# Maxima rows and evacuation moved behind the next round's first exponentials, in the first attention of a two-layer gated cross-attention block

## What is computed

```python
qkv = x @ w_attn + b_attn;  kv_ctx = context_seq @ w_ref + b_ref
key = concat([kc, k], axis=1);  value = concat([vc, v], axis=1)
w = einsum('bhtd,bhsd->bhts', qh, kh) / sqrt(Dh)
...
probs = softmax(w, axis=-1)
a = einsum('bhts,bhsd->bhtd', probs, vh)
```

## Time and profile before

| | |
|---|---|
| median of 3 runs | 696.75 us (691.8 to 701.3) |
| the profiled execution | 700.24 us, span 698.5 us |
| PE busy | 514.7 us (74%) |
| DVE busy | 437.9 us (63%) |
| ACT busy | 298.5 us (43%) |
| mean granted TensorE clock | 0.869 |

### The profile page before, as it was taken

How to read it: one execution, slowest core, us unless ns; L and a number is a source line. 1 busy time by engine, 2 the same in 40 slices (tenths; PEclk the granted TensorE clock), 3 DMA queues, 4 the chain that set the end, 5 groups by cost and what they waited for, 6 DMA issues and landing times. The chain is left out here.

```text
span 698.5 us, 15585 instructions
## 1 busy us (share of the span) xinstructions
PE 514.7 (74%) x5425; PEld 355.1 (51%) x5425; DVE 437.9 (63%) x918; ACT 298.5 (43%) x480; POOL 146.5 (21%) x184
## 2 busy tenths in 40 slices
PE   0381778879878988844537798989975158999994
PEld 0161345556556655733223365655554146788883
DVE  7724577666656676456962676777567873666652
ACT  1065324555555555502404265766753221333331
POOL 1200002111211121100032601112123032444432
PEclk9995968999999897877868788999986578999998
DMA  8030683444534550000044559699447111222310
GB/s 259 4 112 3 117 161 78 127 106 106 124 77 100 145 145 24 2 0 1 0 113 81 150 144 179 138 167 161 136 156 254 54 38 17 42 43 44 51 23 0
DMA packets 73247, 64.31 MB, mean 92 GB/s; under 512 B 33326, under 2 KB 65750, under 8 KB 73190
## 3 DMA queue, kind: packets, MB, share of 16 engines
q1 hardware_dynamic: 61816, 41.78, 26.4%
q0 software_dynamic: 8224, 21.06, 11.6%
q10 hardware_dynamic: 3152, 0.71, 0.5%
HBM read 48.59 MB, written 15.92 MB: 92 GB/s over the span
## 5 line engine op out<-in xcount | busy, mean ns | idle before, releaser
L458 PE MATMUL PS<-QS,KS 112*120 112x100 f16 (+2 forms) x896 | 93.0, 230 | 11.2 <-ACT PT L521 9.5
L458 PEld LDWEIGHTS PS<-QS,KS 112*120 112x120 f16 (+2 forms) x896 | 82.4, 144 | 36.6 <-ACT PT L521 15.1
L569 DVE CUSTOM_DVE_ANT_0 PS<-PS,maskv 100x461 f32<-100x461 f32 x128 | 80.4, 647 | 13.9 <-PE PS L427 12.6
L572 DVE TENSOR_REDUCE mx<-PS 100x1 f32<-100x361 f32 x128 | 63.6, 529 | 37.0 <-PE PS L430 35.8
L521 ACT ACTIVATE PT<-PS 120x400 f32<-120x400 f32 (+1 forms) x128 | 63.3, 503 | 37.1 <-PE PS L458 34.8
L521 ACT ACTIVATE PT<-PS,ctxb 120x400 f32<-120x400 f32 (+1 forms) x96 | 56.9, 594 | 49.8 <-PE PS L458 48.5
L427 PE MATMUL PS<-KS,QS 65*100 65x461 f16 x128 | 51.6, 408 | 15.6 <-DVE mx L569 15.1
L2003 PE MATMUL PS<-WE,hidden_high 128*128 x160 | 55.4, 391 | 5.7 <-issue 5.7
L1990 PE MATMUL PS<-aT,WE 128*128 128x128 f16 x960 | 59.3, 221 | 0.0
L779 POOL TENSOR_SCALAR_AFFINE_SELECT PT<-PT 100x400 f32<-100x400 f32 x32 | 17.7, 554 | 190.8 <-ACT PT L521 190.8
L1990 PEld LDWEIGHTS PS<-aT,WE 128*128 x960 | 56.6, 99 | 0.5
(11 more groups left out here) (302 smaller groups left out, 1062.3 us busy)
## 6 DMA issues: line engine op xcount, KB each, us to landing
share<-in_L_ffn_w_dram POOLq DMA_DIRECT2D x13, 1024.0 KB, 8.5
k_scratch<-share SPq DMA_DIRECT2D x32, 180.5 KB, 2.5
KS<-k_scratch SPq DMA_DIRECT2D x32, 180.5 KB, 3.7
KS<-k_scratch SPq DMA_DIRECT2D x64, 90.2 KB, 5.8
QS<-q_scratch SPq DMA_DIRECT2D x64, 50.0 KB, 2.6
v_scratch<-xn SPq DMA_DIRECT2D x8, 385.7 KB
values_staged<-v_scratch SPq DMA_DIRECT2D x8, 385.7 KB
WE<-in_L_ffn_w_dram POOLq DMA_DIRECT2D x2, 1024.0 KB, 8.8
```

Of the source, the lines that this page charges most:

```text
L458: last = nc.tensor.matmul(bank[0:kn, i * T:(i + 1) * T], KS[p][:, h, k0:k0 + kn], QS[p][:, h, :], start=True, stop=True)
L569: nc.vector.tensor_tensor_reduce(rows, rows, maskv[:, :], 1.0, -BIG, ALU.add, ALU.max, mx[p][:, h:h + 1]).then_inc(s_smf, 1)
L572: nc.vector.tensor_reduce(mx[p][:, h:h + 1], sm_bank[h % 2][0:T, 0:TC], X, ALU.max).then_inc(s_smf, 1)
```

## The change

On ACT the maxima rows of twelve heads move behind the next round's exp0 and the evacuation behind its exp1. `NTURN0` goes from 2 to 3, so that PE's turn and DVE's division stand one step later, and T1 goes from step 3 to step 2 on PE, ACT and DVE (in rounds 0 to 5). ACT's loop gets the form that PE's and DVE's have. No computation is added or removed.

```diff
-        TVK = {1: "T0", 3: "T1", 4: "K0", 5: "K1", 8: "V0", 9: "V1", 11: "K2", 12: "K3"}
+        TVK = {1: "T0", 2: "T1", 4: "K0", 5: "K1", 8: "V0", 9: "V1", 11: "K2", 12: "K3"}
...
-        NTURN0 = 2
+        NTURN0 = 3
...
-                def round0(j, u, keys, nxt, weights=False):
+                def round0(j, u, keys, nxt, first=False, weights=False):
                     nh0 = MISC0 + MISCR * (2 * j + u)
                     for t in range(16):
                         act_exp(act, j, u, t, 0, 0)
+
+                        if t == 0 and not first:
+                            act_max_rows(act, j, u, 1, 0)
+                        if t == 1 and not first:
+                            act_evac(act, j, u - 1, 0)
                         if weights and 1 <= t < 1 + NIB + KC:
                             rounding(NIB + t - 1)
...
                     if nxt:
                         act_max_rows(act, j, u + 1, 0, 0)
-                    act_evac(act, j, u, 0)
-                    if nxt:
-                        act_max_rows(act, j, u + 1, 1, 0)
-
-                with act.Fori(0, B // 2 - 1) as j:
-                    for u in range(2):
-                        round0(j, u, True, True)
+
+                round0(0, 0, True, True, True)
+                with act.Fori(0, B // 2 - 2) as j:
+                    round0(j, 1, True, True)
+                    round0(j + 1, 0, True, True)
+                round0(B // 2 - 2, 1, True, True)
                 round0(B // 2 - 1, 0, False, True)
-                round0(B // 2 - 1, 1, False, False, True)
+                round0(B // 2 - 1, 1, False, False, False, True)
+                act_evac(act, B // 2 - 1, 1, 0)
```

## The result

The changed kernel takes 694.17 us (median of 20 runs, 689.72 to 701.5), the kernel before 699.57 in the same comparison (20 runs, 691.8 to 703.03). The ratio is 0.9947 [0.9921, 0.9972]: 2.0 to 5.5 us faster, well within 2%. The profiled execution took 691.77 us, span 690.0, with a granted clock of 0.869. It lies 8.5 us under the profiled execution before, more than twice the 3.7 us by which the ratio stands under 1. So the two profiles give the mechanism, and the size has to come from many executions.

A forecast was written before the change was run, and what follows sets the result against it. Bound: a seam chain from last PV through four ACT operations, T0's half and five DVE operations to K0. Terms 4.0 + 0.5 + 0.57 + 0.3 - 0.15 = 5.2, plus clock 1.6, make 6.8 us: 690.0 us, range 684 to 697.

The forecast's parts named there:

- the clock's +1.6: Rounds 3 to 5: less PE waiting in the opening removes one of three low-clock stretches, 1.6 us, bounds -3 to 4.7.
- round 6's +0.3: Round 6, without T or K: DVE's wait for the turn holds max2 (0.55), turn 0.3 later; gain 0.3 (0 to 0.5).
- The walk of the seam: Opening of rounds 1 to 5, followed engine by engine: K0 moves from 132.12 to 131.12, full-clock rounds 23.0 instead of 24.0 us.
- the 1.00: Gain per seam at K0: 1.30 us as division and max2 leave its path, less 0.30 for T0's later half.
- T1's wait: PE in the opening: T1 waits about 0.4 us until the twelve heads' rows are read from the bank it overwrites.
- Round 5: Lowest clock (0.87): if low at SM3 already, PE's side binds, so the seam gains 0.5 us (0.3 to 1.0).
- Round 0: No seam, only T1 moved: K0 can follow ST4 by 0.38 instead of 0.95, gain 0.57 us, at least 0.41.
- Round 7: ST2's 1.80 us wait goes, but ST3 and later work wait for later exponentials: loss 0.15 us (0 to 0.3).
- given back later: Rival, chance 0.18: K0 comes earlier but the round's later part is held by something unmoved; gain 0 to 2.5 us, 694 to 697.
- The clock falls more often: Rival, chance 0.10: in the opening, SM3's longer wait brings new low stretches at 1.6 us each; 697 to 701 us.
- Stays high: Rival, chance 0.17: all or most low stretches of rounds 3 to 6 go, gain 10 to 13 us, 684 to 687.
- Fetch stalls: Rival, chance 0.05: ACT's branch ahead of exp0 stalls beyond 0.7 us of cover, costing about 1 us; 691 to 692.

The follow-up runs named there:

- the table alone: Kernel before with only T1 put at step 2 and the turn and division at step 3, ACT's order old: 687.0 and 688.64 us, ratios 0.9808 and 0.9871.
- the ACT part: Kernel before with only ACT reordered: exp0 ahead of the twelve heads' rows, exp1 ahead of the evacuation: 708.79 us, 1.0178.
- fills behind the turn: Changed kernel with four unused 128x512 matmuls behind the turn in rounds 1 to 5: 0.9857, mean 691.4 us; with three more ahead of T1: 0.9906, mean 692.8.
- T1 alone: Kernel before with T1 at step 2, turn and division left at step 2: 0.9931.
- the filled kernel before: Kernel before with eleven unused matmuls in rounds 1 to 5, four ahead of ST2, two of SM3, five of K0: 1.0117, mean 704.2 us.
- the loop form: Kernel before with only ACT's loop rewritten, rounds 0 and 5 written out, its order as before: 0.9981.
- the turn alone: Kernel before with turn and division at step 3, T1 left at step 3: 1.0003.
- six executions with a fill: T1 at step 2, turn and division at step 3, ACT's order old, with four unused matmuls ahead of ST2 in rounds 1 to 5: 0.9799, mean 685.9 us.
- The evacuation back in front: Changed kernel with ACT in the order evacuation, exp0, twelve heads' rows, exp1: 692.56 us, 0.9903, mean 691.1.
- T0's half ahead: Changed kernel with T0's half moved ahead of exp1 and T1's half ahead of exp2 on ACT: 690.17 us, 0.9808, mean 689.2.

## Why the prediction came out as it did

The forecast was faster by 6.8 us with a range of 684 to 697; measured were 694.17 us and some 4 us. The direction and the chain are right. Two terms are not: the clock's +1.6, which measured nothing, and round 6's +0.3, which was -1.0.

- **The walk of the seam** holds. K0 5.2 behind ST0: 5.30 in round 1, 5.19 in round 2. Full-clock rounds of 23.0: 23.0. exp0 0.44 behind ST0: 0.42. T0's half 3.0: 3.01, in part by luck: the rows start 0.53 behind exp0 where I took 0.40, and T0's half 0.39 behind the evacuation (127.20, 127.59) where I took 0.52. T1's remainder directly behind max1, and K0's remainder not held up: both as forecast. Both halves of the 1.00 stand by themselves: the table alone takes 1.27 to 1.30 out of a round (forecast 1.30), and the ACT part gives 0.27 to 0.31 back (forecast 0.30).
- **T1's wait** was forecast as 0.4 and is 0.62. The rows' late start, 0.53 behind exp0 (125.00, 125.53), is most of the difference. K0 did not pay for it: SM3 stands 4.72 behind ST0, where the walk had 4.73, held by max1. Its wait is 0.90 (forecast 1.1), and ST3's (0.1 to 0.2) is not there. The prediction's "other 21 microseconds" of a round are a slip for 18.
- **Round 5**: forecast 0.5, measured 23.01 us at full clock, so 1.0 where the clock holds.
- **Round 0**: forecast 0.57. K0 stands 0.35 behind ST4 where it was 0.95, so 0.60 of it is the walk:

```profile
103.89 0.55 PE L458 MATMUL PS<-QS,KS 112*100 112x100 f16 x4
104.24 0.50 PE L211 MATMUL PS<-cTh,wrh 128*128 128x361 f16 x1
```

 The other 0.8 of the round's 1.4 us is clock, 0.85 against 0.80; the low stretch that lies over its start, and began ahead of it, ends earlier. This goes with T1's place: in all 15 profiles with T1 behind ST2 round 0 takes 24.0 to 25.0 us, in all five with T1 behind ST3 26.0 to 26.5.
- **Round 6** is one step that failed. The prediction has "the turn itself comes some 0.3 later, so 0.3 (0 to 0.5)", with no clock in it. DVE's row is as walked: the division stands there with a wait again, against the earlier trace rows.

```profile
245.14 0.26 DVE L579 RECIPROCAL rden<-PS 100x16 f32<-100x16 f32 x1 [1.05 <-PE PS L495]
```

 But behind this opening the clock falls. The window of the seven microseconds that follow:

```profile
246.00:253.00 7.00, 6.48 (x53) 4.31 (x54) 4.59 (x12) 2.22 (x5) 1.41 (x3) 0.52 0.29 105
```

 A clock of 0.52 is the lower level for almost all of it, and the round loses 1.0. Of ten profiles with exp0 ahead of the twelve heads' rows at this seam and nothing added in round 6, eight show this early stretch (the other two have fills behind the turn in the rounds before); of nine with the old order, two do (T1 alone, and the filled kernel before). So the order makes it likelier; it is not shown to be the whole cause.
- **Round 7**, a loss of 0.15 (0 to 0.3), doesn't show: the span outside rounds 0 to 6 is the same to 0.1 us.

Also as forecast, ST2 in round 7 no longer waits 1.80 but the next ones do:

```profile
266.32 0.42 PE L458 MATMUL PS<-QS,KS 112*120 112x100 f16 x4 [0.37 <-ACT PT L521]
...
268.12 0.42 PE L458 MATMUL PS<-QS,KS 112*120 112x100 f16 x4 [1.38 <-ACT PT L521]
```

- **The clock term** is the step that failed most: "I take it that one of the three stretches goes", +1.6. By the single profile it looks too small, since two of three went. By 44 executions against 108 it is nothing: 0.8659 against 0.8665. With it at zero and round 6 as in the profiles the sum is 5 x 1.0 + 1.4 - 1.0 = 5.4, where the means differ by 4.0 +-1.2. The 1.4 us between them are at the edge of what these executions tell, and no run shows where they went. The rule of the Trainium skill that I cited there (TensorE: Matmul & The Clock Gate, "Part 1: The HAM clock gate"), read as "less waiting, fewer falls", is not what these runs show: PE waits about 1.5 us ahead of K0 both with the whole change (0.62 and 0.90) and with the table alone (1.08 and 0.42), and in rounds 1 to 5 the former has a low stretch in 7 of 15 profiled rounds, the latter in 0 of 15 (two profiles of the table alone, and the one whose order differs only into round 6). The kernels without either gain (before, the loop form, the turn alone), which wait 2.4 to 2.7 us, have 5 of 15.

The rivals: *given back later* is not so in rounds 1 to 5. *The clock falls more often* is true of one place, round 6, and it took back a fifth of the gain; of the ACT part alone it is true everywhere. *Stays high* is, in small, what the table part does without the ACT part (0.8717 against 0.8665, some 2.4 us by the line). *Fetch stalls* are out.

**What bounds the opening** is thus settled: the row of four ACT operations ahead of T0's half, then DVE's row, in the kernel before up to T1's remainder. In the changed kernel K0 waits for nothing, and DVE's row counts only up to max1, which releases SM3; ST4 and K0 follow. The gain is the table's; the ACT part removed PE's largest wait, which was on no chain, and costs 0.3 us a seam and, in round 6, clock. **The best version** seen is the table part alone: mean 688.4, against 694.6 and 698.6. Its six executions with a fill have 685.9, which is not clear of it.

**What stays open** is why waits of the same sum bring low stretches in one arrangement and not in the other. The place (T1's wait and SM3's lie 2.6 us apart, ST2's and SM3's 2.0), the length of each piece, and the kind of matmul between them all changed together. The evacuation back in front has the waits of the changed kernel, 2.2 us apart, and no low stretch in its one profile, but a mean clock like the changed kernel's; the fills leave the same contradiction.

## What to carry to other kernels

Follow the chain back from the instruction that the rest of the round hangs on, and count only what stands in its row on each engine; the largest wait on the busiest engine may be worth nothing, and was here. Where a change has a part that shortens the row and a part that lengthens it, run each alone before both are kept. Where the clock moves by itself, one profile tells which rounds could be short, not how many will be: a term for it belongs in the range, and only the mean clock of many executions gives its size.

## What was not expected of the hardware

- The time of one core's execution moves by more than 10 us with its granted clock: the table part alone took 681.53 us at 0.882 and 692.62 at 0.859.
- One low stretch of a round (mean clock 0.93) costs 1.2 to 1.7 us here: 25.25 and 25.54 against 24.0 before, 24.56 and 24.63 against 23.0 in the changed kernel, 24.09 against 22.4 with T0's half ahead. In rounds 1 to 5 it begins 5 to 8 us behind the four heads' rows.
- On ACT exp1 starts 0.40 after exp0 though exp0 lasts 0.50; the 16x1200 rows behind exp0 start 0.53 behind it, with no overlap.
